# Attention in an adaLN block: the next key tile's first scores move between the two value chunks that begin a head

## The reference

```
sim = einsum('bnkh,bmhk->bnhm', q, k)
attn = softmax(sim / 4, axis=1)            # over n, the queries
o = einsum('bnhm,bmhv->bnhv', attn, v)     # sum over m, the keys
out = einsum('bnhv,dhv->bnd', o, output_proj)
```

## Time and profile before

| what | us or share |
|---|---|
| median of three runs | 1684.09 |
| profiled execution, its span | 1685.73, 1684.4 |
| TensorE matmuls busy | 1640.7 (97%) |
| VectorE busy | 1578.9 (94%) |
| ScalarE busy | 1374.7 (82%) |
| GpSimd busy | 779.4 (46%) |
| granted TensorE clock, mean | 0.996 |
| maxima (L1073), mean of 1024 | 1.213 |
| exponentials (L825), mean of 1024 | 1.113 |

### The profile page before, as it was taken

How to read it: one execution, slowest core, us unless ns; L and a number is a source line. 1 busy time by engine, 2 the same in 40 slices (tenths; PEclk the granted TensorE clock), 3 DMA queues, 4 the chain that set the end, 5 groups by cost and what they waited for, 6 DMA issues and landing times.

```text
span 1684.4 us, 38849 instructions
## 1 busy us (share of the span) xinstructions
PE 1640.7 (97%) x15454; PEld 817.2 (49%) x15454; DVE 1578.9 (94%) x1705; ACT 1374.7 (82%) x2508; POOL 779.4 (46%) x1625
## 2 busy tenths in 40 slices
PE   9999999999999999999999999999999999999998
PEld 8743333333333333673333333333333379999997
DVE  7899999999999999769999999999999879888887
ACT  5599999999999999569999999999999833333332
POOL 3034445444444545303454544566654457555542
PEclk8999999999999999999999999999999999999999
DMA  6102111112111112511111121111112533534420
GB/s 232 65 9 72 51 49 46 45 50 67 52 51 51 46 45 76 168 38 45 46 45 45 45 70 50 52 51 46 46 45 64 157 113 126 155 125 155 145 67 19
DMA packets 83110, 123.15 MB, mean 73 GB/s; under 512 B 4713, under 2 KB 69105, under 8 KB 82929
## 3 DMA queue, kind: packets, MB, share of 16 engines
q1 hardware_dynamic: 82512, 120.15, 22.5%
q10 hardware_dynamic: 416, 0.53, 0.1%
HBM read 74.52 MB, written 46.15 MB: 72 GB/s over the span
## 4 chain that ended last, share of the span: by engine, by line
DVE 64%; PE 32%; issue 2%; ACT 1%; POOL 1%; DMA 0%; POOLq 0%; DVEq 0%
DVE nm L1073 60%; PE acc L447 13%; PE slot L447 10%; PE acc L615 6%; PE slot L671 1%; PE slot L586 1%; DVE ost L1086 1%; ACT e_sb L825 1%; PE slot L468 0%; PE acc L646 0%; DVE qs L1140 0%; DMA v_sb<-in_x 0%; DVE e_sb L1128 0%; DVE e_sb L1147 0%; PE slot L494 0%
## 5 line engine op out<-in xcount | busy, mean ns | idle before, releaser
L1073 DVE TENSOR_REDUCE nm<-slot 128x1 f32<-128x1024 f32 x1024 | 1166.1, 1213 | 20.2 <-PE slot L586 18.0
L825 ACT ACTIVATE e_sb<-slot,nm 128x1024 f32<-128x1024 f32 x1024 | 1137.6, 1113 | 17.5 <-DVE nm L1073 12.5
L615 PE MATMUL acc<-e_sb,vp 64*64 64x512 f32 x8192 | 1060.7, 594 | 6.3 <-DVE ost L1086 4.7
L586 PE MATMUL slot<-stq,stk 64*64 64x512 f16 x4096 | 411.6, 388 | 21.6 <-ACT e_sb L825 21.6
L586 PEld LDWEIGHTS slot<-stq,stk 64*64 64x64 f16 x4096 | 117.6, 103 | 626.5 <-ACT e_sb L825 592.7
L615 PEld LDWEIGHTS acc<-e_sb,vp 64*64 64x64 f32 x8192 | 283.3, 132 | 188.1 <-issue 73.8
L1309 POOL TENSOR_TENSOR dlt<-nm 128x4 f32<-128x4 f32 x128 | 25.8, 202 | 408.2 <-DVE nm L1073 408.2
L825 ACT ACTIVATION_READ_ACCUMULATOR e_sb<-slot,nm 128x1 f32 x1024 | 199.8, 195 | 0.0
L1300 POOL TENSOR_TENSOR vp<-v_sb,fac 128x512 f32<-128x512 f32 x128 | 133.6, 1044 | 10.2 <-POOL fac L1290 0.3
L1286 POOL TENSOR_TENSOR rtot<-tot,mone 128x4 f32<-128x4 f32 x128 | 132.8, 1038 | 10.0
L1280 POOL TENSOR_TENSOR wsum<-cor,ssum 128x8 f32<-128x8 f32 x128 | 26.0, 203 | 233.7 <-ACT cor L855 233.7
(11 more groups left out here) (180 smaller groups left out, 1931.5 us busy)
## 6 DMA issues: line engine op xcount, KB each, us to landing
o_r<-o_heads SPq DMA_DIRECT2D x32, 1024.0 KB, 7.2
stk<-qk_parts SPq DMA_DIRECT2D x128, 128.0 KB
o_heads<-ost_hi SPq DMA_DIRECT2D x64, 256.0 KB, 3.4
o_heads<-ost SPq DMA_DIRECT2D x64, 256.0 KB, 4.1
v_sb<-in_x SPq DMA_DIRECT2D x16, 512.0 KB, 6.1
qk_parts<-e_sb SPq DMA_DIRECT2D x32, 256.0 KB, 2.3
stq<-qk_parts SPq DMA_DIRECT2D x128, 64.0 KB
out<-e_sb SPq DMA_DIRECT2D x32, 128.0 KB, 1.8
```

The costliest lines, as they stand in the source:

```text
L586: mm = pe.matmul(slot[s][side * VD:(side + 1) * VD, c * 512:(c + 1) * 512], stk[c * 64:c * 64 + 64, h % 2, i * P + side * VD:i * P + (side ...
L615: mm = pe.matmul(acc[half * VD:(half + 1) * VD, c * 512:(c + 1) * 512], vp[rows, g % 3, gi, half, :], e_v[rows, j % ERING, n0:n0 + 512], s ...
L825: act.activation(e_v[:, j % ERING, half * 1024:(half + 1) * 1024], slot[u % 3][:, :], ACT.Exp, bias=nm[:, g % 4, i, half:half + 1], accum_ ...
L1073: dve.tensor_reduce(nm[:, g % 4, i, half:half + 1], slot[u % 3][:, :], AX.X, ALU.max, negate=True).then_inc(maxed.sem)
```

## The change

In the iteration that begins a head (L709), the first scores of the next tile are issued between the two `attend` calls, and the next iteration (`begun`) leaves them out:

```diff
                     begins = jv > 0 and jv % NT == 0
+                    begun = jv > 1 and jv % NT == 1
                     for half in range(2):
-                        if j < JT:
+                        if j < JT and not (begun and half == 0):
                             scores(b, j, half)
                         if jv >= 0 and not begins:
                             attend(b, 2 * jv + half)
                     if begins:
                         attend(b, 2 * jv)
+                        if j + 1 < JT:
+                            scores(b, j + 1, 0)
                         attend(b, 2 * jv + 1)
```

## The result

| | before | after |
|---|---|---|
| median of five runs each | 1684.32 us | 1692.82 us |
| lowest to highest | 1681.34 to 1685.68 | 1692.33 to 1697.89 |
| span of the profiled execution | 1684.4 | 1691.0 |

The ratio is 1.0057, with a 95% interval of 1.0046 to 1.0068: 8.5 us more, where 11.1 were forecast; the median is 1692.82, and 1695.2 was forecast.

What follows compares the result with a forecast made beforehand. VectorE's maxima were taken to bound each head, with small stalls at its beginning. A 0.13 us wait plus 0.24 us of scores, 0.37 per head, times 30 gave 11.1 us: 1695.2 us forecast, range 1688 to 1699.

Steps and rivals of the forecast that it cites:

- The bound and the pattern: Attention: VectorE's maxima at 1.13 us bound each head, period 37.00 us, 30 times; 0.19 us stalls at each head's beginning.
- The moved scores wait 0.13: Behind A0, the moved scores wait for their slot, held by a ScalarE exponential; TensorE idles 0.13 us per head.
- They cost 0.24 in front of A1: On TensorE, A1 starts 0.24 us behind the moved scores; with their wait, 0.37 us later than before.
- In their old place they were free: Between A1 and A2, S(j+1,0) ran in time that A2 had to wait for A1 anyway, so it cost nothing.
- A2 starts 0.71 behind A1's last round: On TensorE, A2 waits for A1's completion and still starts 0.71 us after A1's last round, without scores between.
- Rival 1: A2 is released after A1's recorded 0.589 us, not 0.71; loss 0.25 us per head, 7.5 us, 1691.6; 9%.
- rival 2: A2 isn't held by A1 at all; price 0.04 us per head, 1.2 us, 1685.3, no change; 10%.
- Nothing gives it back: Inside a head VectorE works without a gap, so the 0.37 us per head is not recovered later.
- The total wait of A2's kind: Sign: the total wait of TensorE's loads released by "PE acc L615" grows by about 30 x 0.3 us.
- rival 4: ScalarE falls behind as tile j+1's first exponential waits for A2; 0.11 us more per head, 14.4 us, 1698.5; 6%.
- rival 3: Neither moved scores nor A2 wait; the second maximum comes 0.09 us earlier per head, 2.7 us gain, 1681.4; 3%.
- The sum: Over 30 heads, 0.37 us each gives 11.1 us: 1696.8 for the profiled execution, 1695.2 us for the median.

Runs made afterwards that it cites:

- e6: The changed kernel with ScalarE's half of the copy of acc given to VectorE, which makes both; copy to copy 37.82 us, one execution 1706.56 us.
- e3: The changed kernel with the four matmuls of the moved scores made twice, in the new place; copy to copy 37.57 us, one execution 1701.55 us.
- e4: The kernel before with the four matmuls of S(j+1,0) made twice in their old place between A1 and A2; copy to copy 37.175 us, one execution 1688.59 us.

## Why the prediction was right

- **The bound and the pattern.** Right. Each of the 30 heads changed by the same 0.36, and nothing inside a head changed.
- **The moved scores wait 0.13.** Right: they start 1.83 after the copy, where 1.82 was forecast (432.82 - 430.99), behind ScalarE's accumulator read; e6 takes it away, and 0.13 of the stall goes. Unrounded the wait is 0.137.
- **They cost 0.24 in front of A1.** Right: A1 0.24 behind them; e3 shows that a group there counts in full.
- **In their old place they were free.** Right: A2's load came 0.71 behind A1's last round with one group of scores between them (before), with two (e4) and with none (e6). The second group cost 0.09 of its 0.215.
- **A2 starts 0.71 behind A1's last round.** 0.70: A1's second round is at 433.06 + 0.43 = 433.49, and A2's load is at 434.18. Unrounded it is 0.696, and before it was 0.714. The scores between are not what made it longer, since e6 has 0.714 without them. What differs is the round itself: in the kernel before, in e4 and in e6 three of its four matmuls start 0.036 behind the first, and in the changed kernel all four start together. With these 0.02 less, and a slot wait of 0.137 for 0.13, the sum is 0.36 instead of 0.37 per head. Rival 1, 0.59, falls with these rows, and rival 2, no wait at all, falls as well. The Trainium skill ("TensorE: Matmul & The Clock Gate", Single matmul latency) gives a lone matmul about 166 ns over its streaming; the estimate from it is 0.43 + 0.17 = 0.60, and the trace has 0.70. What makes the other 0.10 was not taken apart.
- **Nothing gives it back.** Right: the stretch inside a head has the old pace.
- **The total wait of A2's kind.** Of the signs named this is the one that missed: 13.5 us more, where about 30 x 0.3 = 9 were given. The wait itself came as forecast; the idle time before the load grew by more, because the scores' load no longer stands in it.
- **ScalarE (rival 4).** The wait came as worked out: the exponential of S(j+1,0) starts at 435.40, released by TensorE, where 435.29 + 0.09 was forecast, 30 times and 6.8 us in all. It cost nothing, because the next maximum ended later than ScalarE was free.
- **Gain (rival 3).** Did not come. Even e6, whose scores wait for no slot, has the wait between A1 and A2 behind them.
- **The sum.** 30 x 0.361 = 10.8 for 11.1. The measured 8.5 is smaller by what differs outside attention. In the two traces that is 4.2 us, in stretches where the execution of before had a lower clock; that it is the same in the medians is likely, but not shown. I scaled the forecast from the profiled execution to the median and did not ask what clock its opening stretch had been granted, though the mean of 0.996 stood in the table. That is the one step missing.

## What to carry to other kernels

Work that stands between two dependent instructions on one queue may be free because of where it stands; before moving it, look for a releaser on the engine's own name in the loads behind it. A move has two ends: what it now waits for at the new place (here a slot that comes free 0.13 later, with the whole queue behind), and what its old place now lays bare. Where an engine on the chain works without a gap afterwards, a delay of a few tenths once per head is paid in full each time, and a gain for the first item means nothing if the second one is later.

## What the runs showed of the hardware

- A group of f32 matmuls with a dependent load behind it: 0.70 to 0.71 us from the start of the last round to that load, whether no other matmuls, four or eight of them stood between (e6, before, e4), and 0.43 from round to round without a dependency. After such a wait the second round follows the first after 0.48 instead of 0.43 (434.18 to 434.67).
- In executions of one and the same kernel on one core the mean clock runs from 0.995 to 1.000, and the time with it: before 1681.81 at 1.000 and 1687.38 at 0.995. In the two traces compared above the difference lay in stretches outside attention. Differences of 0.2% are better read from the period of the repeating part.
